# Moving the row normalisation of a macaron FFN-attention block from VectorE to ScalarE, with the order of the work refitted

## The chip, the cores and the metric

The kernel runs on one core of a Trainium2 chip. The metric is the device time of one launch in microseconds (us); of the kernel before there are three runs. Engines are named as in the profile: PE is TensorE, DVE VectorE, ACT ScalarE, POOL GpSimd, SP SyncE, which issues the transfers. L12 is line 12 of the kernel before, unless the text says that it is of the changed one.

## What is computed

The input x is 4 x 2048 x 256 float32. Three residual blocks follow one another, and each begins with a layer norm of the rows of x:

```python
x = x + 0.5 * ffn(layernorm(x), w_gate, w_up, w_down)
x = x + attention(layernorm(x), Wq, Wk, Wv, Wproj, lq1, lk1, lq2, lk2)
x = x + 0.5 * ffn(layernorm(x), w_gate, w_up, w_down)
# layernorm(x) = (x - mean) * rsqrt(var + eps), per row of 256
# ffn: every linear layer quantises input and weights to FP4 (E2M1) in
# blocks of 16: scale = max|x|/6, round x/scale to the grid, times scale;
# hidden size 704, silu(gate) * up
# attention: causal, 8 heads, two softmaxes per head whose difference
# (first - lam * second) weighs the values; q and k are RMS-normed and
# rotated, the output of a head is layer-normed
```

## The kernel before, in words

**Tiles.** A tile is 128 rows of x, a pair is two tiles, a chunk is four (512 rows). There are 16 chunks, four for each batch. The kernel makes four passes over a chunk: 0 is the first FFN, 1 the projections to q, k and v, 2 the output projection of attention, 3 the second FFN. `xb` holds five chunks of x; the load of chunk c+5 goes into the room of chunk c once that is stored. Weights are quantised, transposed and split into float16 high and low parts in a prologue, into which the first stages of chunk 0 are woven.

**From x to the matmul (passes 0, 1 and 3).** For a chunk, DVE makes mean and variance (`stats`, L1089 and L1092), POOL the reciprocal root (`rstd`, L905 to L916, six small steps on 128x4, once for a chunk and pass, 48 times). Then for each pair DVE writes the normed rows into `xq` (`norm_a`, L1104, two instructions of 128x256, one for each tile; 96 pairs, 192 instructions). In the FFN passes, the FP4 stages follow: `scale_x` on DVE (L1063, L1066, L1068), `divide_x` on POOL (L896), `square_x` on ACT (L979), `grid_x` and `points_x` on DVE (L1145, L1150), `dequant_x` on POOL (L923), and in all three passes `high_x` on ACT and `low_x` on POOL (L992, L930), and the transposing DMA `turn_x` from SP (L875). PE multiplies with the weights (L1299, `hidden`), ACT makes the tanh (L969), DVE the gate (L1122 to L1133), the hidden tile goes through the same FP4 stages (`hq`), PE multiplies again (L1312, `down`), and DVE adds to x (L1157).

**Attention.** For each chunk and each of four groups of heads: scores on PE (L1336), exp on ACT (L1036, two per step of 128 keys), on the diagonal a mask on POOL (L956), values on PE (L1354). Scores have two rooms of two PSUM banks each, or three for the (group, chunk) pairs listed in `WIDE`.

**What sets the order.** Every engine runs its own stream in order. A list scheduler, `Plan.order`, writes these streams when the kernel is built: at each step it places the stage that can start first, ties and near ties being settled by the table `DUE` (a due time for each kind of stage and each chunk). Its model has a cost for each kind (`COST`), gaps between a stage and the next (`LATE`, `AFTER`), and the stages in `PORT`, for which it lets DVE and POOL wait for one another. So every change of a cost or of `DUE` can move every stage on every engine; dependencies are kept by semaphores whatever the order. The model's numbers are no measurement, and none is used here.

**Lines to follow.** `norm_a` is added to DVE's stream in `quantise` (L435) and for pass 1 (L499), and run at L1093. SP's `store` is L862, its `load` L854, and before the load SP waits for the store of that room to have landed.

## Time and profile before

| what | value |
|---|---|
| time, median of 3 runs | 2159.77 us (2158.83 to 2162.08) |
| time of the profiled execution | 2159.3 us |
| span of the profiled execution | 2157.6 us |
| instructions | 39254 |
| granted TensorE clock, mean | 0.975 of 2.4 GHz |
| PE, DVE, ACT, POOL busy | 1878.2, 1688.2, 1626.0, 1351.2 us |
| L1104 on DVE | 192 instructions, 152.4 us |

The span runs from the first instruction to the last; the time adds what lies around it, here 1.7 us. Busy times are those of one execution, with overlaps counted once, and a DVE or POOL instruction that is held up after it has begun counts as busy. That is why a shape that always does the same work can have very different durations.

### The profile page before, as it was taken

What the parts mean: (1) busy time and instruction counts of PE and PEld (TensorE: products, weight loads), DVE (VectorE), ACT (ScalarE), POOL (GpSimd) and SP (SyncE); (2) the same over time, 40 slices, a digit from 0 to 9 for tenths busy, and PEclk for the clock granted to TensorE, in tenths of its full rate; (3) what the DMA queues carried; (4) which work ended last, traced back from release to release, by engine and by line L of the source; (5) the groups of instructions that cost most, each with busy time, mean ns of one, the idle gap of its engine ahead of it and who ended that gap; (6) DMA issues with size and microseconds to landing.
All of it is one profiled execution on the core that took longest, in us unless ns stands there. A gap on an engine that the chain in (4) does not pass through costs nothing. (4 is left out here: it accounts for less than half of the span.)

```text
span 2157.6 us, 39254 instructions
## 1 busy us (share of the span) xinstructions
PE 1878.2 (87%) x13634; PEld 785.1 (36%) x13634; DVE 1688.2 (78%) x3516; ACT 1626.0 (75%) x2339; POOL 1351.2 (63%) x1343
## 2 busy tenths in 40 slices
PE   1766999998999898999998999999999889999965
PEld 1332434343333342444332333444442424342223
DVE  8899898897845899889954999998976769841285
ACT  2334888877887788787889788777878778889942
POOL 6677776766645676776753677876764656641154
PEclk9898999999999999999999999999999989999988
DMA  4123543425221445332421444333521342320013
GB/s 125 31 54 69 86 82 63 87 44 93 49 48 35 71 68 103 61 85 46 79 58 24 73 78 86 62 72 71 90 46 43 59 79 55 72 48 17 11 33 70
DMA packets 477492, 136.15 MB, mean 63 GB/s; under 512 B 458224, under 2 KB 477040, under 8 KB 477296
## 3 DMA queue, kind: packets, MB, share of 16 engines
q1 hardware_dynamic: 477296, 133.65, 32.6%
q8 instruction: 110, 1.80, 0.4%
q14 instruction: 86, 0.70, 0.1%
HBM read 11.96 MB, written 8.39 MB: 9 GB/s over the span
## 5 line engine op out<-in xcount | busy, mean ns | idle before, releaser
L1036 ACT ACTIVATE probs<-psum 128x1024 f32<-128x1024 f32 (+3 forms) x1280 | 1071.7, 918 | 113.7 <-PE psum L1336 91.7
L1354 PE MATMUL psum_o<-probs,v_sb 128*32 128x512 f32 (+3 forms) x5120 | 570.3, 541 | 16.6 <-POOL probs L956 13.7
L1299 PE MATMUL psum<-w_gu_T,xT 128*128 128x512 f16 (+1 forms) x2304 | 507.7, 369 | 58.1 <-DVE qscale L1066 14.7
L1336 PE MATMUL psum<-q_stack,k_stack 64*128 64x512 f16 (+3 forms) x2560 | 386.6, 353 | 78.3 <-ACT probs L1036 59.5
L1299 PEld LDWEIGHTS psum<-w_gu_T,xT 128*128 128x128 f16 x2304 | 212.6, 99 | 331.6 <-issue 58.0
L1312 PE MATMUL psum<-w_down_T,hT 128*128 128x256 f16 x2176 | 269.1, 280 | 40.0 <-DMA hT<-h 14.1
L956 POOL TENSOR_SCALAR_AFFINE_SELECT probs<-probs 128x512 f32<-128x512 f32 x256 | 179.7, 709 | 160.3 <-ACT probs L1036 159.3
L1336 PEld LDWEIGHTS psum<-q_stack,k_stack 64*128 64x128 f16 x2560 | 99.4, 93 | 486.9 <-ACT probs L1036 374.1
L923 POOL TENSOR_TENSOR hq<-grid,qscale 128x704 f32<-128x704 f32 x128 | 187.0, 1462 | 126.2 <-DVE grid L1150 126.2
L969 ACT ACTIVATE hq<-psum,tanh_scale 128x512 f32<-128x512 f32 (+1 forms) x256 | 144.0, 563 | 150.9 <-PE psum L1299 143.6
L1312 PEld LDWEIGHTS psum<-w_down_T,hT 128*128 128x128 f16 x2176 | 210.6, 100 | 107.5 <-issue 31.1
L930 POOL TENSOR_TENSOR h<-hq,h 128x704 f16<-128x704 f32 x128 | 202.6, 1583 | 67.6 <-ACT h L992 67.2
L896 POOL TENSOR_TENSOR hq<-hq,rscale 128x704 f32<-128x704 f32 x128 | 188.6, 1474 | 78.8 <-DVE rscale L1068 78.3
L1354 PEld LDWEIGHTS psum_o<-probs,v_sb 128*32 128x32 f32 x5120 | 117.7, 109 | 245.5 <-issue 167.2
L930 POOL TENSOR_TENSOR x<-xq,x 128x512 f16<-128x512 f32 x128 | 160.6, 1256 | 69.0 <-ACT x L992 68.8
L1145 DVE SCALAR_TENSOR_TENSOR hq<-grid,hq 128x704 f32<-128x704 f32 x128 | 145.0, 1135 | 31.3 <-ACT grid L979 30.2
L1104 DVE TENSOR_SCALAR xq<-xb,mean_var,rstd 128x256 f32<-128x256 f32 x192 | 152.4, 841 | 17.4 <-POOL rstd L916 17.0
L1323 PE MATMUL psum<-w_qkv_T,xT 128*128 128x512 f16 (+1 forms) x768 | 144.4, 335 | 24.5 <-DMA xT<-x 8.4
L1150 DVE SCALAR_TENSOR_TENSOR grid<-grid,hq 128x704 f32<-128x704 f32 x128 | 149.8, 1173 | 0.7
L992 ACT ACTIVATE h<-hq 128x704 f16<-128x704 f32 x128 | 102.2, 798 | 47.1 <-POOL hq L923 34.4
L979 ACT ACTIVATE grid<-hq 128x704 f32<-128x704 f32 x128 | 101.7, 798 | 37.9 <-POOL hq L896 37.3
L1157 DVE SCALAR_TENSOR_TENSOR xb<-psum,down_scale,xb 128x256 f32<-128x256 f32 x128 | 58.9, 461 | 80.6 <-PE psum L1312 80.3
(118 smaller groups left out, 2319.4 us busy)
## 6 DMA issues: line engine op xcount, KB each, us to landing
xb<-L_attn_x SPq DMA_DIRECT2D x16, 512.0 KB, 4.0
out<-xb SPq DMA_DIRECT2D x16, 512.0 KB, 3.1
xT<-x SPq DMA_TRANSPOSE x128, 3.1
hT<-h SPq DMA_TRANSPOSE x128, 3.5
k_stack<-st SPq DMA_TRANSPOSE x64, 3.2
q_stack<-st SPq DMA_TRANSPOSE x64, 3.3
k_stack<-L_ffn_w_down SPq DMA_DIRECT2D x1, 704.0 KB, 4.1
k_stack<-L_ffn_w_gate SPq DMA_DIRECT2D x1, 512.0 KB, 5.2
```

Source lines behind the costliest of these rows:

```text
L896: nc.gpsimd.tensor_tensor(by_block(a), by_block(a), rscale[:, i, 0:nb].unsqueeze(2).broadcast_to([P, nb, QB]), ALU.mult).then_inc(scaled_r ...
L923: nc.gpsimd.tensor_tensor(by_block(a), by_block(g), qscale[:, i, 0:nb].unsqueeze(2).broadcast_to([P, nb, QB]), ALU.mult).then_inc(quantise ...
L930: nc.gpsimd.tensor_tensor(low, buffers(kind, key)[0], high, ALU.subtract)\
L956: nc.gpsimd.affine_select(out=blk, in_=blk, compare_op=ALU.is_ge, fill=0.0, base=0, pattern=[[0, 4], [1, P]], channel_multiplier=-1)\
L1036: nc.scalar.activation(probs[:, s % 3, 2 * u:2 * u + 2, q0:CHUNK], psum[:, plan.pairs[s, u]:plan.pairs[s, u] + 2, q0:CHUNK], ACT.Exp, scal ...
L1104: last = nc.vector.tensor_scalar(a[:, j * C:(j + 1) * C], xb[:, t % XB, :], mean_var[:, slot, i, 0:1], rstd[:, slot, i:i + 1], ALU.subtrac ...
L1145: nc.vector.scalar_tensor_tensor(a, g, GRID_BASE, a, ALU.add, ALU.add).then_inc(grid_ready, 1)
L1150: nc.vector.scalar_tensor_tensor(points(e[1], e[2:]), g, GRID_BASE, a, ALU.add, ALU.subtract)\
L1299: last = nc.tensor.matmul(bank(e)[:, 0:hi - lo], xs[:, x, t % 2, k, :], w_gu_T[:, w, k, lo:hi], start=n == 0, stop=n == len(parts) - 1)
L1312: last = nc.tensor.matmul(bank(e)[:, 0:C], hs[0:n, k, :], w_down_T[0:n, w, :], start=i == 0, stop=i == len(parts) - 1)
L1336: last = nc.tensor.matmul(psum[:, plan.pairs[s, u] + j, q0:CHUNK], k_stack[half, at, h, kt % NTC * P:(kt % NTC + 1) * P], q_stack[half, c ...
L1354: last = nc.tensor.matmul(psum_o[at:at + VD, q0:CHUNK], v_sb[:, kt // NTC % SLOTS * NTC + kt % NTC, 2 * g + u, :], probs[:, s % 3, 2 * u + ...
```

## The change

The norm becomes two ACT instructions with a scale and a bias per row: `x * rstd + offset`, where `offset = -mean * rstd` is made by POOL in two added steps of 128x4 after `rstd`. In `rstd`, the last product is no longer the end: a semaphore `mean_negated` counts the negated means, `early_rstd` the rstd, and `rstd_ready` is given after the offset. `scale_x` on DVE and `high_x` on ACT wait for `early_normed` as before, now counted in ACT's order.

In the scheduler: `norm_a` is on "scalar" with a cost of 1090 instead of 540, out of `PORT`, and the second pair of a chunk is also said to need the first; `rstd` costs 3400 instead of 2780; a load that follows a store on SP is counted from the end of the store (`AFTER`), where it was counted from the end of its issue. `WIDE` has 43 pairs of group and chunk instead of 35, and all rows of `DUE` have new numbers. In the prologue, the four norms of chunk 0 stand before ACT's third weight square instead of before DVE's `scale_x`.

```diff
 DUE = {
...
-WIDE = {0: (1, 5, 8, 9, 10, 12, 13, 14, 15), 1: (0, 1, 2, 3, 5, 6, 7, 13, 14, 15), 2: (3, 6, 8, 9, 11, 13, 14, 15), 3: (1, 5, 7, 10, 11, 13, 14, 15)}
+WIDE = {0: (1, 2, 3, 5, 6, 7, 10, 13, 14, 15), 1: (1, 2, 3, 4, 5, 6, 8, 11, 13, 14, 15), 2: (0, 2, 3, 5, 7, 9, 11, 12, 13, 14, 15), 3: (1, 2, 3, 4, 6, 7, 9, 10, 11, 13, 15)}
...
-            mask=640, norm_a=540, norm_heads=690, norm_qk=685, points_h=890, points_x=690,
+            mask=640, norm_a=1090, norm_heads=690, norm_qk=685, points_h=890, points_x=690,
...
-            read_v=470, rms=4170, rope=1940, rope_add=1270, rstd=2780, scale_x=1295, square_h=795,
+            read_v=470, rms=4170, rope=1940, rope_add=1270, rstd=3400, scale_x=1295, square_h=795,
...
-         ("head_stats", "norm_heads"): 35, ("rope", "rms"): 35, ("norm_a", "scale_x"): 35}
+         ("head_stats", "norm_heads"): 35, ("rope", "rms"): 35, ("store", "load"): 50, ("norm_a", "scale_x"): 35}
...
-            dequant_h=0, low_h=0, rope_add=0, low_qk=0, mask=0, norm_a=0)
+            dequant_h=0, low_h=0, rope_add=0, low_qk=0, mask=0)
...
-            add(norm, "vector", at("norm_a"), needs, takes, frees)
+            add(norm, "scalar", at("norm_a"), needs, takes, frees)
...
-            quantise("x", pair, [("rstd", *stats)], [("xu", pair)], [("stats", stats)] if i else [])
+            quantise("x", pair, [("rstd", *stats), ("norm_a", "x", pas, pair[1] - 1) if i else None], [("xu", pair)], [("stats", stats)] if i else [])
...
-                    nc.gpsimd.tensor_tensor(rstd[:, slot, :], t, y, ALU.mult).then_inc(rstd_ready, 1)
+                    n, o = EARLY_RSTD[e], offset[:, slot, :]
+                    nc.gpsimd.tensor_scalar(o, mean_var[:, slot, :, 0], -1.0, None, ALU.mult)\
+                        .then_inc(mean_negated, 1)
+                    nc.gpsimd.tensor_tensor(rstd[:, slot, :], t, y, ALU.mult).then_inc(early_rstd, 1)
+                    pool.wait_ge(mean_negated, n + 1)
+                    pool.wait_ge(early_rstd, n + 1)
+                    nc.gpsimd.tensor_tensor(o, o, rstd[:, slot, :], ALU.mult).then_inc(rstd_ready, 1)
...
+                    for j in range(2):
+                        t = 2 * p + j
+                        i = t % NTC
+                        last = nc.scalar.activation(a[:, j * C:(j + 1) * C], xb[:, t % XB, :], ACT.Identity,
+                                                    bias=offset[:, slot, i:i + 1], scale=rstd[:, slot, i:i + 1])
+                    last.then_inc(early_normed, 1)
...
-                        last = nc.vector.tensor_scalar(a[:, j * C:(j + 1) * C], xb[:, t % XB, :],
-                                                       mean_var[:, slot, i, 0:1], rstd[:, slot, i:i + 1],
-                                                       ALU.subtract, ALU.mult)
-                    last.then_inc(early_normed, 1)
...
-                    vector_stages(dve, first["norm_a"] + first["scale_x"])
+                    vector_stages(dve, first["scale_x"])
...
+                        if i == 2:
+                            scalar_stages(act, first["norm_a"])
```

**Where it moves instructions.** ACT in the prologue: the first stages of the kernel. L1744 and, in the changed kernel, L1756 are the squares of the three weight matrices, L1003 is the norm. Before:

```order
L1744 ACT_TABLE_LOAD
L1744 ACTIVATE probs<-k_stack 128x1536 x3
L979 ACTIVATE psum<-xq 128x512 x2
L1754 ACTIVATE w_gu_T<-psum,hq 128x512 x2
L1754 ACTIVATE w_gu_T<-psum,hq 128x192 x2
```

and in the changed kernel:

```order
L1756 ACT_TABLE_LOAD
L1756 ACTIVATE probs<-k_stack 128x1536 x2
L1003 ACTIVATE xq<-xb,offset,rstd 128x256 x4
L1756 ACTIVATE probs<-k_stack 128x1536
L990 ACTIVATE psum<-xq 128x512 x2
```

The four norms of chunk 0 now stand between the second and the third square. ACT's stream has one table load in either kernel.

DVE in 54:216, at the second chunk. `hq<-hq,psum` is the gate, `psum<-xq` to `rscale<-qscale` is `scale_x`, `hq<-grid,hq` and `grid<-grid,hq` are the grid steps of a hidden tile. Before:

```order
L1104 TENSOR_SCALAR xq<-xb,mean_var,rstd 128x256 x2
L1122 SCALAR_TENSOR_TENSOR hq<-hq,psum 128x512
L1145 SCALAR_TENSOR_TENSOR hq<-grid,hq 128x704
L1127 SCALAR_TENSOR_TENSOR hq<-hq,psum 128x512
L1150 SCALAR_TENSOR_TENSOR grid<-grid,hq 128x704
L1063 TENSOR_REDUCE psum<-xq 128x32
L1066 TENSOR_SCALAR qscale<-psum 128x32
L1068 RECIPROCAL rscale<-qscale 128x32
```

and in the changed kernel:

```order
L1132 SCALAR_TENSOR_TENSOR hq<-hq,psum 128x512
L1088 TENSOR_REDUCE psum<-xq 128x32
L1091 TENSOR_SCALAR qscale<-psum 128x32
L1093 RECIPROCAL rscale<-qscale 128x32
L1088 TENSOR_REDUCE psum<-xq 128x32
L1091 TENSOR_SCALAR qscale<-psum 128x32
L1093 RECIPROCAL rscale<-qscale 128x32
L1155 SCALAR_TENSOR_TENSOR hq<-grid,hq 128x704
L1137 SCALAR_TENSOR_TENSOR hq<-hq,psum 128x512
```

The norm is gone from the stream, and `scale_x`, which waits for it, stands directly behind gate steps, with grid steps of a hidden tile behind it. On PE, 72 of the 768 projection matmuls (L1323) and 234 of the 2304 `hidden` ones stand ahead of the first scores before, 96 and 264 in the changed kernel.

SP around the first store (`out<-xb`) and load (`xb<-L_attn_x`). Before:

```order
L875 DMA_TRANSPOSE xT<-x 128x8x128
L862 DMA out<-xb 128x4x256
L854 DMA xb<-L_attn_x 128x4x256
L875 DMA_TRANSPOSE xT<-x 128x8x128 x3
L875 DMA_TRANSPOSE hT<-h 128x11x128 x2
```

and in the changed kernel:

```order
L880 DMA_TRANSPOSE xT<-x 128x8x128
L867 DMA out<-xb 128x4x256
L880 DMA_TRANSPOSE xT<-x 128x8x128
L859 DMA xb<-L_attn_x 128x4x256
L880 DMA_TRANSPOSE xT<-x 128x8x128 x3
```

One transposition has come between the two. This is so for one of the 11 loads before and for five in the changed kernel.

## Rows read from the trace of the kernel before

**Rows 1.** The page: busy time, share of the span, instructions of each engine.
```profile
PE 1878.2 (87%) x13634; PEld 785.1 (36%) x13634; DVE 1688.2 (78%) x3516; ACT 1626.0 (75%) x2339; POOL 1351.2 (63%) x1343
```

**Rows 2.** Windows of the span: start and end, length, busy us per engine, PEclk, DMA.
```profile
54.00:216.00 162.00, 108.80 (x522) 54.29 (x522) 148.73 (x295) 63.88 (x110) 113.21 (x114) 0.85 0.27 51
216.00:2052.00 1836.00, 1696.25 (x12712) 690.07 (x12712) 1418.93 (x3018) 1515.98 (x2158) 1145.12 (x1145) 0.99 0.34 63
2052.00:2158.00 106.00, 63.52 (x366) 33.22 (x362) 75.33 (x138) 32.01 (x52) 55.19 (x48) 0.85 0.25 53
1944.00:2052.00 108.00, 99.07 (x800) 27.92 (x798) 22.12 (x63) 104.42 (x129) 17.33 (x26) 1.00 0.06 14
```

**Rows 3.** Windows of L1104 alone: start and end, length, DVE busy (x count).
```profile
54.00:216.00 162.00, 23.13 (x24) 0.85 0.27 51
216.00:2052.00 1836.00, 121.47 (x160) 0.99 0.34 63
540.00:702.00 162.00, 9.18 (x12) 1.00 0.21 43
1620.00:1728.00 108.00, 6.79 (x10) 0.98 0.26 52
1944.00:2052.00 108.00, 1.38 (x4) 1.00 0.06 14
```

**Rows 4.** L1104: durations in ns, least, median, most.
```profile
L1104 DVE TENSOR_SCALAR xq<-xb,mean_var,rstd x192: 315/718/2995, 24.0 to 2091.4; 128x256 f32<-128x256 f32 x192
```

**Rows 5.** Timeline at 807: start, duration, engine, line [idle before it <- releaser].
```profile
807.37 4.25 DVE L1104 TENSOR_SCALAR xq<-xb,mean_var,rstd 128x256 f32<-128x256 f32 x4 [0.29 <-POOL rstd L916]
808.33 1.33 POOL L935 TENSOR_TENSOR roped<-roped,rope_b 128x512 f32<-128x512 f32 x1
813.67 1.47 PE L1323 MATMUL psum<-w_qkv_T,xT 128*128 128x512 f16 x6 [2.42 <-DVE qscale L1066]
```

**Rows 6.** Lines on ACT: count, busy us, mean ns; then two in a row (timeline).
```profile
L1758 ACT ACTIVATE w_qkv_T<-hq 128x256 f16<-128x256 f32 x2 | 0.7, 406 | 0.0
L979 ACT ACTIVATE psum<-xq 128x512 f32<-128x512 f32 x64 | 39.6, 619 | 32.6 <-POOL xq L896 22.9 <-DVE rope_b L1181 3.8 <-DVE hq L1122 1.7
L1007 ACT ACTIVATE rope_b<-psum,att_scale 128x512 f32<-128x512 f32 x64 | 44.2, 691 | 28.6 <-POOL roped L935 15.4 <-PE psum L1323 13.1
L1754 ACT ACTIVATE w_proj_T<-psum,hq 128x256 f16<-128x256 f32 x2 | 0.9, 474 | 0.0
...
59.07 0.87 ACT L1754 ACTIVATE w_proj_T<-psum,hq 128x256 f16<-128x256 f32 x2
```

**Rows 7.** Lines on POOL: the first step of rstd.
```profile
L905 POOL TENSOR_SCALAR var<-mean_var 128x4 f32<-128x4 f32 x48 | 14.7, 307 | 81.7 <-DVE mean_var L1092 79.6
```

**Rows 8.** Timeline of the prologue, POOL, ACT and DVE.
```profile
17.93 1.64 POOL L916 TENSOR_TENSOR rstd<-root_t,root 128x4 f32<-128x4 f32 x1
22.36 1.48 ACT L1744 ACTIVATE probs<-k_stack 128x1536 f32<-128x1536 f32 x1 [5.28 <-POOL k_stack L1534]
23.97 3.96 DVE L1104 TENSOR_SCALAR xq<-xb,mean_var,rstd 128x256 f32<-128x256 f32 x4
```

**Rows 9.** Waits of PE in 216:2052: us in total, times, longest.
```profile
PE psum L1336 <- ACT probs L1036: 58.8, 138, 1.4
PE psum_o L1354 <- POOL probs L956: 13.3, 22, 1.6
PE psum L1336 <- DVE hq L1133: 5.6, 4, 2.2
```

**Rows 10.** Waits of SP and of DVE for the transfers of a chunk.
```profile
SPq L854 <- DMA out<-xb: 27.2, 11, 2.8
DVE stat L1089 <- DMA xb<-L_attn_x: 29.1, 10, 6.7
```

**Rows 11.** Timeline of the tail: the last four norms.
```profile
2087.89 3.86 DVE L1104 TENSOR_SCALAR xq<-xb,mean_var,rstd 128x256 f32<-128x256 f32 x4
```

**Rows 12.** L1036, the exps: durations in ns, first and last start.
```profile
L1036 ACT ACTIVATE probs<-psum x1280: 362/1021/1369, 212.1 to 2057.2; 128x1024 f32<-128x1024 f32 x128, 128x512 f32<-128x512 f32 x21, 128x256 f32<-128x256 f32 x17, 128x768 f32<-128x768 f32 x17
```

More of the change, by code:

```diff
@@ L498, in whole_plan @@
                 norm = ("norm_a", "x", *pair)
-                add(norm, "vector", of_pair("norm_a", *pair), [("rstd", 1, c), ("norm_heads", "x", 2, NTC * (c - 2) // 2 - 1) if c >= 3 else None],
+                add(norm, "scalar", of_pair("norm_a", *pair), [("rstd", 1, c), ("norm_a", "x", 1, pair[1] - 1) if i else None,
+                     ("norm_heads", "x", 2, NTC * (c - 2) // 2 - 1) if c >= 3 else None],
                     [(rings_of(*pair)[0], pair)], [("stats", (1, c))] if i == NTC - 2 else [])
@@ L696, in macaron_kernel @@
         early_normed = sem("early_normed")
+        mean_negated = sem("mean_negated")
+        early_rstd = sem("early_rstd")
         bank_full = [sem(f"bank_full{i}") for i in range(BANKS)]
@@ L739, in macaron_kernel @@
         QUANT = ordinals(order["vector"], ("quant_h", "scale_x"))
-        EARLY_NORM = ordinals(order["vector"], ("norm_a",))
+        EARLY_NORM = ordinals(order["scalar"], ("norm_a",))
+        EARLY_RSTD = ordinals(order["gpsimd"], ("rstd",))
         DIVIDE = ordinals(order["gpsimd"], ("divide_x", "divide_h"))
@@ L980, in scalar_stages @@
                         .then_inc(full(e)[0] if e[1] == "x" else square_done, 1)
+                elif e[0] == "norm_a":
+                    pas, p = e[2:]
+                    slot = STAT[pas, 2 * p // NTC] % STATS
+                    a = buffers("x", (pas, p))[0]
+                    before = last_low("x", (pas, p))
+                    if before:
+                        act.wait_ge(low_ready, before)
+                    act.wait_ge(rstd_ready, RSTD["rstd", pas, 2 * p // NTC] + 1)
+                    for j in range(2):
[4 more added lines that the diff above has]
+                    last.then_inc(early_normed, 1)
                 elif e[0] in ("high_x", "high_h"):
@@ L1092, in vector_stages @@
                         nc.vector.bn_aggr(mean_var[:, slot, i, :], stat6[:, i, :]).then_inc(var_ready, 1)
-                elif e[0] == "norm_a":
-                    pas, p = e[2:]
-                    slot = STAT[pas, 2 * p // NTC] % STATS
-                    a = buffers("x", (pas, p))[0]
-                    before = last_low("x", (pas, p))
-                    if before:
-                        dve.wait_ge(low_ready, before)
-                    dve.wait_ge(rstd_ready, RSTD["rstd", pas, 2 * p // NTC] + 1)
-                    for j in range(2):
-                        t = 2 * p + j
-                        i = t % NTC
-                        last = nc.vector.tensor_scalar(a[:, j * C:(j + 1) * C], xb[:, t % XB, :],
-                                                       mean_var[:, slot, i, 0:1], rstd[:, slot, i:i + 1],
-                                                       ALU.subtract, ALU.mult)
-                    last.then_inc(early_normed, 1)
                 elif e[0] == "scale_x":
```

63 lines of the change are left out of this document (32 added, 31 removed), and 136 rows, old and new, of the table DUE.

## The prediction

> **What bounds the kernel now.** I read the page's busy line first [rows 1]: PE 87%, DVE 78%, ACT 75%, POOL 63% of 2157.6 us. No engine is full over the whole span, so the question is which is full where. The windows answer it [rows 2]. Up to 54 us the weights are prepared. In 54:216 the first chunks go through the MLP with no attention beside it: DVE is busy 148.73 of 162 us (92%), PE 108.80 (67%), ACT 63.88 (39%), POOL 113.21 (70%). That stretch is DVE's. In 216:2052 attention and MLP run side by side: PE 1696.25 of 1836 us (92%), ACT 1515.98 (83%), DVE 1418.93 (77%). PE is nearest to full, and its 140 us of idle time are what can be won. In 2052:2158 the last MLP chunks drain through hand-offs between all engines, DVE 75.33 of 106 us.
>
> The operation that moves is L1104. It costs DVE 23.13 us in 54:216 and 121.47 us in 216:2052 [rows 3], 3.96 us for four in the prologue [rows 8] and 3.86 us for four in the tail [rows 11], 152.4 us in all, 794 ns of DVE time for each of the 192. Its single durations are 315 ns at least, 718 at the median, 2995 at most [rows 4], for one shape. What stretches it is seen at 807.37 [rows 5]: four of them take 4.25 us while POOL runs additions from SBUF one after another, and PE's projection at 813.67 has stood 2.42 us for a DVE step queued behind them. Advanced Engine Details and Errata in the Trainium skill (VectorE Performance Modes) says that VectorE's second SBUF port is shared with GpSimd and that two-port instructions and GpSimd's block each other. The trace agrees: the same 256 elements take 315 ns or over 1 us, beside a busy POOL.
>
> **The change, part by part.**
>
> *DVE loses L1104*: 192 instructions, 152.4 us.
>
> *ACT gains 192 ACTIVATEs* with a scale and a bias read from SBUF. The trace has none with two such operands. From below: 128x256 with neither takes 406 ns [rows 6]. Each operand: at 128x512, none takes 619 ns and one takes 691 [rows 6], so 72 ns. Two give 406 + 144 = 550 ns. Two in a row overlap: a pair of one-operand 128x256 takes 0.87 us where one takes 474 ns [rows 6], so 0.08 us less than the sum. A pair is then 2 x 0.55 - 0.08 = 1.02 us, 96 pairs 98 us. From both sides: 0.81 us a pair without any surcharge (78 us), and 1.38 us, the price of the one-operand 128x512 twice (133 us). I take 98, since the shape and the surcharge both have a row. ACT goes from 1626 to 1724 us (80%). ScalarE: Activation LUTs in the Trainium skill (What ACT_TABLE_LOAD costs) has 186 ns + 0.833 ns per element and 93 ns per pointer operand, which would be 585 ns for one; an estimate by it is about 5 us more over the kernel.
>
> *POOL gains two steps per chunk and pass*, 48 x 2 instructions of 128x4, as L905 is (307 ns) [rows 7]: 96 x 0.307 = 29 us, 0.6 us each time. POOL is busy 63% and its order is packed around other waits, so nothing of this is on the path, except that a norm's operands come some 0.6 us later. If POOL were full, it would cost the 29 us.
>
> *Prologue.* L1104 ran at 23.97 for 3.96 us, although rstd was there at 19.57 [rows 8]: DVE was in its weights until then. ACT had stood idle for the 5.28 us before 22.36. The new order puts the four norms ahead of ACT's third weight square: 19.6 + 0.6 + 2.0 = 22.2, about when that square is released. DVE can go on to the scaling steps 3.9 us sooner. After it DVE waits for POOL's weights in part; I count 2 of the 3.9 us.
>
> *54:216.* DVE's work falls by 23.1 us, from 148.7 to 125.6. If DVE kept its 13.3 us of idle time, the stretch would be 23 us shorter. But a norm is now a hand-off, POOL to ACT to DVE, and scale_x on DVE waits for it with gate and grid steps queued behind. ACT has the room: 63.9 us and 12 pairs are 76 us. I let DVE's idle time grow by half, 13.3 to 20: the stretch becomes 146 us, **16 us less**. Bounds: 0 and 23. PE's order now has 96 instead of 72 projection matmuls ahead of its first scores (in the section on the change), so this is not bought by leaving work for later; it only means that the first exp comes less early than the stretch shrinks.
>
> *216:2052.* PE's 140 us of idle time: 58.8 before scores for ACT and 13.3 for POOL's mask [rows 9]; the other 67.7 lie in small groups, most of them waits for DVE, the largest 5.6 us. DVE's load here falls from 77% to 71%, and the 4 us blocks as in [rows 5] vanish. I take a quarter of the 67.7, **17 us less**; bounds 0 and 67.7. Against it, 80 pairs, 82 us, enter ACT, which goes from 83% to 87%. Where ACT is the bound they show in full. The pure case is 1944:2052, ACT 104.42 of 108 us [rows 2]. With the other stretches that are thin in MLP, 12 norms in 540:702, 10 in 1620:1728, 4 in 1944:2052 [rows 3] and as many in 1080:1188, these are 30 norms, 15 pairs, **15 us more**. Elsewhere the exps have slack and I count none; if that cover is gone, it is the rival below. The new WIDE table gives three rooms of scores to 43 of 64 head groups of a chunk, where it was 35. PE's 58.8 us arise when both rooms wait for ACT, and if they came from the 29 narrow ones in equal parts, 8 of them turning wide would save 16 us. A third room doesn't make ACT faster, so I take a quarter, **4 us less**.
>
> *Store and load.* SP stood 27.2 us in 11 waits of the load for the store before it, and DVE 29.1 us in 10 waits for the rows of x [rows 10]. The new order places a transposition between the two in 5 of 11 cases, 1 before. The DVE waits lie in PE's busy middle. I count 0; bounds 0 and 5 us less.
>
> *Tail.* Four norms took 3.86 us on DVE, of which the first pair, half of it, stood ahead of everything that follows [rows 11]. Now 0.6 us on POOL and one pair of 1.02 us on ACT stand there; DVE is also free for its other steps: **1 us less**.
>
> **Sum:** 2 + 16 + 17 - 15 + 4 + 1 = 25 us less. The profiled execution has a span of 2157.6 us and a time of 2159.3, 0.5 below the median of 2159.8. I predict **2135 us**. What a measurement of this kernel can tell from no change is about 0.2%, 4 us.
>
> **The rivals.**
>
> *ACT becomes the bound (slower).* In 216:2052 each pair stands in ACT's order among exps with a median of 1.02 us [rows 12], and PE has two or three rooms of scores. A norm that has become ready late holds the exps behind it. For it: the scores already wait 58.8 us for ACT [rows 9]. Against: ACT is idle 320 us there. If all 80 pairs reach PE, that is 82 us more instead of 15. Break-even with my gains of 40 us is at half of them. At 60% they cost 49 us against those 40, which makes **2169 us**. By the rule of ScalarE: Activation LUTs (Rules for kernel authors), plain multiplies and adds belong on VectorE. By the shortest row, 315 ns, the move would indeed trade 192 x 0.315 = 60 us of DVE for 98 us of ACT; then 8 us would go from 54:216 in place of 23, and this rival would be the likeliest. The 794 ns of DVE time that each takes in these rows speak against the rule here.
>
> *The gain is given back (no change).* PE is 92% busy in the middle; its idle time may move from DVE's account to ACT's, and what the head wins is lost while chunks wait for their place. Head 18, middle -15, refitted order neither way: **2157 us**.
>
> *DVE was worse than it looks (much faster).* All of 23 + 4 in the head, half of the 67.7 in the middle, and ACT's pairs hidden: 61 us, **2099 us**.
>
> *The change doesn't do what it says.* A second function on ACT might force table loads. ACT's order has one table load, as before. I give this nothing.
>
> **How the numbers follow.** Forecast (2120 to 2152) 0.54; no change (2151 to 2164) 0.19, of which 0.07 lie below 2155.5; slower 0.16 (up to 2185); much faster (below 2120) 0.11. The range that leaves out about a fifth, a little of the slow side and most of the very fast: 2112 to 2166. Faster 0.72, same 0.12, slower 0.16.
>
> **What would show it.** Right: DVE near 1536 us and ACT near 1724; norms on ACT near 550 ns with little spread; the first exp, at 212.1 now [rows 12], near 195; PE's waits for DVE in the middle well below 60 us in sum. Wrong: the first exp comes no earlier (then DVE wasn't the head's bound); PE's wait for ACT before scores well above 75 us (the slower rival); POOL above 1400 us, or DVE idle before L1088 for ACT by tens of us (the hand-off is dearer than I have it).

## The result, and the profile after

The changed kernel takes 2111.47 us (median of 4 runs, 2110.53 to 2114.67), beside 2160.93 us for the kernel before on the same chip. The ratio is 0.9773, 95% interval 0.9756 to 0.979: 49.5 us less, where 25 were forecast. The time lies just under the range that was given. The profiled execution took 2114.67 us with a span of 2112.9; it was the longest of the four.

The page of the changed kernel, its busy line, answers to [rows 1]:

```profile
PE 1863.1 (88%) x13634; PEld 784.6 (37%) x13634; DVE 1550.5 (73%) x3324; ACT 1706.1 (81%) x2531; POOL 1374.2 (65%) x1439
```

DVE has lost 137.7 us, ACT has 80.1 more, POOL 23.0 more. PE's count is the same; its busy time is 15.1 us less, and its idle time fell from 279.4 to 249.8 us. Both together make the 44.7 us between the spans. PE's granted clock was higher, 0.983 in the mean of the span against 0.975, and its busy time is shorter in the same ratio (0.992 both). So a third of the 44.7 us is PE's own time for the same matmuls.

Windows of the changed kernel, columns as in [rows 2] (the last one ends with the kernel):

```profile
54.00:216.00 162.00, 118.66 (x646) 59.35 (x644) 148.19 (x308) 85.77 (x151) 135.05 (x137) 0.89 0.33 61
216.00:2052.00 1836.00, 1692.41 (x12716) 692.71 (x12715) 1323.44 (x2889) 1583.97 (x2324) 1162.38 (x1236) 0.99 0.35 63
2052.00:2113.00 61.00, 39.05 (x218) 22.75 (x215) 37.52 (x62) 17.04 (x26) 34.27 (x25) 0.84 0.36 73
```

In 54:216 DVE is as full as before (148.19 against 148.73 us). The relief was not turned into idle time: PE did 646 matmuls in that stretch, where it did 522. DVE is still the fullest engine of the head, it only gets more done there. The granted clock was 0.89 where it had been 0.85.

The lines that answer to [rows 4, 12], durations in ns and first and last start, then the norm's line with its busy time and mean:

```profile
L1003 ACT ACTIVATE xq<-xb,offset,rstd x192: 583/599/887, 21.7 to 2050.6; 128x256 f32<-128x256 f32 x192
L1061 ACT ACTIVATE probs<-psum x1280: 361/1024/1330, 204.9 to 2021.2; 128x1024 f32<-128x1024 f32 x128, 128x512 f32<-128x512 f32 x21, 128x256 f32<-128x256 f32 x17, 128x768 f32<-128x768 f32 x17
...
L1003 ACT ACTIVATE xq<-xb,offset,rstd 128x256 f32<-128x256 f32 x192 | 105.4, 618 | 21.1 <-POOL offset L927 14.7 <-POOL x L941 6.2
```

One norm lasts 599 ns at the median, 583 at least. Norms that follow one another overlap, so the 192 take 105.4 us together. They overlap with ACT's other instructions too, so ACT's busy time rose by 80.1 us only; in the same way DVE lost 152.4 us of norms and 137.7 of busy time. The spread of [rows 4] (315 to 2995 ns) is gone. The exps start 7.2 us earlier (204.9 against 212.1) and end 36.0 us earlier (2021.2 against 2057.2).

PE's waits in 216:2052, the rows that answer to [rows 9] (us in total, times, longest), and one of DVE over the whole span:

```profile
PE psum L1346 <- ACT probs L1061: 62.0, 129, 1.6
PE psum_o L1364 <- POOL probs L967: 10.6, 21, 1.7
PE psum L1309 <- DVE hq L1143: 4.7, 3, 3.0
...
DVE psum L1088 <- ACT xq L1003: 48.8, 13, 16.4
```

The scores wait for ACT little more than before (62.0 against 58.8 us), although 164 norms now stand in ACT's order in that stretch. All rows of that view with DVE as the releaser sum to 33.1 us, 48.2 before, and all with ACT to 68.2, 60.5 before. The window is the same for both kernels, but in the changed one it takes in 31 us behind the last exp; the next paragraph compares equal work instead. DVE itself stands 48.8 us for the norms in 13 waits, 16.4 us the longest: the new hand-off.

**Where the 44.7 us of the span arise.** I compare the two traces where PE has done the same amount of matmul work (each kind of matmul counted with its mean duration of before). The changed kernel is ahead by 3.6 us at PE's first `hidden` matmul (58.8 against 62.4), by 20.7 where the kernel before stands at 216 us (17 to 23 in the 40 us around it, since the two orders differ), by 36.1 at 2058 us, just behind the last exp, and by 44.7 at the end. The stretches of equal work between these points, columns as in [rows 2], the kernel before first:

```profile
59.40:215.90 156.50, 103.62 (x496) 50.51 (x496) 145.49 (x287) 58.52 (x97) 111.57 (x110) 0.85 0.28 53
215.90:2057.80 1841.90, 1701.24 (x12759) 691.37 (x12757) 1421.70 (x3024) 1521.78 (x2168) 1149.18 (x1150) 0.99 0.34 63
2057.80:2157.60 99.80, 58.63 (x324) 32.00 (x316) 72.56 (x132) 26.21 (x42) 51.23 (x43) 0.84 0.27 56
```

```profile
55.80:195.20 139.40, 97.58 (x499) 49.40 (x499) 127.82 (x264) 69.64 (x122) 117.66 (x123) 0.88 0.32 58
195.20:2021.70 1826.50, 1693.32 (x12757) 693.23 (x12754) 1315.90 (x2863) 1587.52 (x2328) 1163.32 (x1230) 1.00 0.35 63
2021.70:2112.90 91.20, 57.86 (x320) 31.58 (x316) 64.07 (x129) 27.82 (x45) 50.74 (x44) 0.88 0.31 61
```

So 3.6 us come up to the first `hidden` matmul, 17.1 in the head behind it, 15.4 in the 1840 us of the middle and 8.6 in the tail. In the middle PE's waits for DVE fell from 48.2 to 22.4 us and those for POOL from 13.3 to 10.0; its waits for ACT rose from 61.2 to 69.2 and those for transfers from 8.1 to 15.7; short gaps and waits for nothing that the profile shows are 5.8 us more; its own time fell by 7.9 us, at a granted clock of 1.00 against 0.99. In the tail PE's waits for transfers fell from 22.2 to 13.9 us. PE's waits there, two rows of the kernel before and the largest of the changed one:

```profile
PE psum L1299 <- DMA xT<-x: 11.3, 2, 7.0
PE psum L1312 <- DMA hT<-h: 10.9, 3, 5.5
...
PE psum L1322 <- DMA hT<-h: 13.9, 4, 4.8
```

### The profile page after: what moved, and what is told of

Same layout as the page of the kernel before. It is cut to its first block and busy times, and to the rows that moved or that the text cites. A ratio compares the mean times of both kernels' runs of the same rounds, so it can differ in the third digit from the quotient of the medians.

```text
span 2112.9 us, 39423 instructions
## 1 busy us (share of the span) xinstructions
PE 1863.1 (88%) x13634; PEld 784.6 (37%) x13634; DVE 1550.5 (73%) x3324; ACT 1706.1 (81%) x2531; POOL 1374.2 (65%) x1439
## 5 line engine op out<-in xcount | busy, mean ns | idle before, releaser
L1346 PE MATMUL psum<-q_stack,k_stack 64*128 64x512 f16 (+3 forms) x2560 | 384.8, 352 | 81.8 <-ACT probs L1061 62.4
L1309 PEld LDWEIGHTS psum<-w_gu_T,xT 128*128 128x128 f16 x2304 | 213.7, 99 | 314.0 <-issue 48.2
L980 ACT ACTIVATE hq<-psum,tanh_scale 128x192 f32<-128x192 f32 (+1 forms) x256 | 143.0, 561 | 106.7 <-PE psum L1309 105.5
L901 POOL TENSOR_TENSOR hq<-hq,rscale 128x704 f32<-128x704 f32 x128 | 187.5, 1466 | 62.5 <-DVE rscale L1093 62.0
L941 POOL TENSOR_TENSOR x<-xq,x 128x512 f16<-128x512 f32 x128 | 156.5, 1226 | 77.7 <-ACT x L1017 77.4
L1333 PE MATMUL psum<-w_qkv_T,xT 128*128 128x512 f16 (+1 forms) x768 | 141.9, 331 | 13.6 <-DVE xb L1167 6.6
L1167 DVE SCALAR_TENSOR_TENSOR xb<-psum,down_scale,xb 128x256 f32<-128x256 f32 x128 | 59.8, 468 | 105.2 <-PE psum L1322 104.7
L1003 ACT ACTIVATE xq<-xb,offset,rstd 128x256 f32<-128x256 f32 x192 | 105.4, 618 | 21.1 <-POOL offset L927 14.7
```

Source lines behind the costliest of these rows:

```text
L901: nc.gpsimd.tensor_tensor(by_block(a), by_block(a), rscale[:, i, 0:nb].unsqueeze(2).broadcast_to([P, nb, QB]), ALU.mult).then_inc(scaled_r ...
L941: nc.gpsimd.tensor_tensor(low, buffers(kind, key)[0], high, ALU.subtract)\
L980: nc.scalar.activation(buffers("h", h[1:3])[0][:, lo:hi], bank(h)[:, 0:hi - lo], ACT.Tanh, scale=tanh_scale[:, 0:1]).then_inc(tanh_done, 1)
L1309: last = nc.tensor.matmul(bank(e)[:, 0:hi - lo], xs[:, x, t % 2, k, :], w_gu_T[:, w, k, lo:hi], start=n == 0, stop=n == len(parts) - 1)
L1346: last = nc.tensor.matmul(psum[:, plan.pairs[s, u] + j, q0:CHUNK], k_stack[half, at, h, kt % NTC * P:(kt % NTC + 1) * P], q_stack[half, c ...
```

## The experiments

The experiments are built on both kernels with one thing changed: each of the 384 transposing DMAs is a plain copy of the same tile, so the products that follow work on untransposed data. `plain_b4` and `plain_a4` are these two bases; the others change one of them further. Where an order is said to be kept, the planner runs unchanged and the result is edited after it, so every other instruction keeps its place on its engine. The kernel before, run beside each group of experiments, took 2159.1 to 2160.6 us, so times of different groups can be compared to some 2 us.

### The bases

```
-  sp.dma_start_transpose(to, halves(kind, key)...)
+  sp.dma_start(to, halves(kind, key)...)
```

> The kernel before with each of the 384 transposing transfers replaced by a plain copy of the same tile, so that rows are not transposed and the output isn't the reference's; nothing else changes. It is the base of the experiments. If the plain copies land within 1 us of the 3.1 to 3.5 us of the transposing ones, the time stays within 1% of 2161 us.

> The changed kernel with the same replacement. If the transposing transfers play no part in the gain, its ratio to the kernel before with plain copies is 0.977 within 0.004, as for the two whole kernels. If they do, the ratio is above 0.985 or below 0.969.

Measured: 2155.27 us (10 runs, ratio to the kernel before 0.998, 0.997 to 0.9989) and 2101.68 us (ratio 0.9731, 0.9712 to 0.9749). The step between them, 53.6 us or a ratio of 0.975, is that of the change within its interval, so the bases stand for the two kernels. The transposing transfers are not quite without a part: PE's waits for transfers in 216:2052 rise by 7.6 us (8.1 to 15.7) with the change in the whole kernels and by 2.9 (1.3 to 4.2) in the bases, about as much as the gain of the bases is larger.

### What a norm costs on each engine, alone and beside POOL

A program of its own: 12 norms on DVE alone, 12 beside POOL's multiplications of 128x512, 24 on ACT of which the last 12 beside POOL, and 12 bn_stats on DVE beside POOL.

> A small program in place of the kernel: twelve norms of 128x256 on DVE alone, twelve POOL products of 128x512 alone, both together, twelve norms on ACT alone and beside POOL, and twelve statistics of 128x256 on DVE beside POOL. If the 794 ns of a norm on DVE come from POOL's instructions, it is under 350 ns alone and near the length of a POOL instruction beside them, while the statistics and the norm on ACT (583 ns at least in the changed kernel) keep their times beside POOL. If not, all keep their times.

The timeline of this program (start, duration of the group, line, count):

```profile
8.91 3.96 DVE L73 TENSOR_SCALAR dve_out<-xb,pair 128x256 f32<-128x256 f32 x12 [8.91 <-DMA xb<-L_attn_x]
13.02 29.96 POOL L56 TENSOR_TENSOR pool_out<-pa,pb 128x512 f32<-128x512 f32 x24 [11.27 <-DVE dve_out L73]
27.74 15.39 DVE L73 TENSOR_SCALAR dve_out<-xb,pair 128x256 f32<-128x256 f32 x12 [14.87 <-POOL pool_out L56]
...
44.53 12.05 ACT L92 ACTIVATE act_out<-xb,pair 128x256 f32<-128x256 f32 x24
...
65.35 4.02 DVE L82 BATCH_NORM_STATS2 stat_out<-xb 128x6 f32<-128x256 f32 x12 [22.22 <-POOL pool_out L56]
```

A norm on DVE takes 330 ns alone (3.96 / 12) and 1283 ns beside POOL (15.39 / 12), where one POOL multiplication follows another every 1268 ns: one norm gets through for each POOL instruction. Two batches of 12 on POOL took 29.96 us with the norms beside the second, and a batch without any takes 14.70: POOL loses 0.56 us on 12, or 4%. ACT's norms come every 502 ns (12.05 / 24) with or without POOL. bn_stats on DVE, over the same 256 elements, takes 4.02 us for 12 beside POOL, about what 12 norms take alone. So ACT's price is steady, and DVE's depends on what POOL does.

### Each half of the change alone, the order kept

`act_old_order` is the kernel before in its own order, with each norm moved from DVE's list into ACT's at the start that the plan had for it, and POOL's two steps added. `dve_new_order` is the reverse: the changed kernel in its own order, each norm back in DVE's list, POOL's two steps kept.

```
   order = plan.order()
+  moved = [e for e in order["vector"] if e[0] == "norm_a"]
+  order["vector"] = [e for e in order["vector"] if e[0] != "norm_a"]
...
+  to = order["scalar"]
...
+  for e in moved:
+      if e not in LEAD:
+          n = next((i for i, o in enumerate(to) if o not in LEAD and plan.start[o] > plan.start[e]), len(to))
+          to.insert(n, e)
```

> Plain copies; the kernel before with every engine's order kept, only the 192 norms taken out of DVE's stream and put into ACT's at their planned times, with POOL's two added steps. Theory relief (the gain is DVE's 152 us of norms, off an engine that sets the pace in the head and holds others for 2 to 4 us at a time in the middle): most of the gain is there without any refit, 28 to 50 us below the kernel before with plain copies. Theory refit (the new DUE and WIDE tables carry the gain, wherever the norm runs): within 12 us of it. A third, that norms between exps only pay with an order that allows for them: 5 us or more above it, and PE's wait for ACT before scores well above 62 us.

> Plain copies; the changed kernel with every engine's order kept, only the 192 norms taken out of ACT's stream and put into DVE's at their planned times (POOL's two added steps stay). Theory relief: the gain is lost, 40 us or more above the changed kernel with plain copies, DVE busy above 1690 us. Theory refit: within 15 us of it.

Measured: act_old_order 2158.92 us (10 runs), ratio 0.9999 to the kernel before, 0.9988 to 1.0009; that is 3.7 us above its base. dve_new_order 2209.75 us, ratio 1.0229: 108 us above its base. Neither the move nor the order alone gains anything. Theory relief, most of the gain without any refit, is refuted by the first run. Theory refit has the time of the first run (within 12 us) and is refuted by the second (within 15 us was its figure). The third has the mechanism, 87.6 us of waits where it said well above 62, and its time is short of it, 3.7 us for 5 or more.

| | order of before | new order |
|---|---|---|
| norm on DVE | 2155.3 | 2209.8 |
| norm on ACT | 2158.9 | 2101.7 |

PE's largest waits in 216:2052, first of the base of before, then of act_old_order, then of the base of after, then of dve_new_order:

```profile
PE psum L1336 <- ACT probs L1036: 57.6, 137, 1.4
PE psum_o L1354 <- POOL probs L956: 12.8, 21, 1.6
PE psum L1336 <- DVE hq L1133: 5.6, 4, 2.2
PE psum L1323 <- DVE qscale L1066: 5.5, 4, 2.4
```

```profile
PE psum L1356 <- ACT probs L1071: 87.6, 165, 3.5
PE psum_o L1374 <- POOL probs L977: 9.5, 16, 1.3
PE psum_o L1374 <- ACT probs L1071: 6.3, 8, 1.8
PE psum L1319 <- DVE hq L1142: 3.2, 5, 2.0
```

```profile
PE psum L1346 <- ACT probs L1061: 61.7, 127, 1.7
PE psum_o L1364 <- POOL probs L967: 10.2, 21, 1.7
PE psum L1309 <- DVE hq L1143: 5.0, 3, 3.0
```

```profile
PE psum L1372 <- ACT probs L1072: 50.5, 104, 2.9
PE psum L1335 <- DVE qscale L1102: 13.0, 9, 4.9
PE psum L1372 <- DVE qscale L1102: 10.7, 6, 3.3
```

Summed over all rows of this view, PE's waits in 216:2052 stand as follows: for DVE 53.3 us in the base of before, 27.4 in act_old_order, 40.1 in the base of after, 103.0 in dve_new_order; for ACT 59.5, 97.7, 65.7 and 55.5. (Of the 40.1 us only 25.8 lie ahead of the last exp, at 2008.9.) In the old order the move took 26 us of waits for DVE away and put 38 us of waits for ACT in their place. The new order has the one with little of the other. PE's own time for the same matmuls counts as well: 1888.1 us in the base of before, 1886.3, 1862.7 and 1889.8, at granted clocks of 0.970, 0.971, 0.981 and 0.967. These 25 us are part of the 59 between the two bases' spans (2157.0 and 2098.1); the move alone or the order alone has none of them.

The old order did gain in the head. Its exps as the trace's lines have them, the base of before and act_old_order:

```profile
L1036 ACT ACTIVATE probs<-psum x1280: 366/1022/1383, 213.1 to 2058.8; 128x1024 f32<-128x1024 f32 x128, 128x512 f32<-128x512 f32 x21, 128x256 f32<-128x256 f32 x17, 128x768 f32<-128x768 f32 x17
```

```profile
L1071 ACT ACTIVATE probs<-psum x1280: 361/1023/1383, 199.2 to 2067.4; 128x1024 f32<-128x1024 f32 x128, 128x512 f32<-128x512 f32 x21, 128x256 f32<-128x256 f32 x17, 128x768 f32<-128x768 f32 x17
```

It is 13.9 us ahead at the first exp and 8.6 us behind at the last one. The lead was 8.9 us at the 240th exp and gone by the 480th.

### Only the head's norms on ACT

```
+  on_act = lambda e: at_chunk[e[2], 2 * e[3] // NTC] < HEAD_NS     # 216000
-  moved = [e for e in order["vector"] if e[0] == "norm_a"]
+  moved = [e for e in order["vector"] if e[0] == "norm_a" and on_act(e)]
```

> The order of the kernel before as it was, plain copies for the transposes, and only the 32 normalisations planned before 216 us moved to ACT (with POOL's two extra steps for every chunk); the other 160 stay on DVE. With all 192 moved at this order (act_old_order) the first exponential came 13.9 us earlier (199.2 against 213.1), and the whole was 3.7 us slower. Theory A (in the head the relief of DVE is worth its full size, and the loss comes behind the head, where ACT's exponentials stand between PE's scores and products): the first exponential near 199, PE's waits for ACT from 216 to 2052 near 60 us as with the norm on DVE and not near 98, and the program near 2141, 14 us below plain_b4's 2155.3. Rival B (an order laid out for a late head gives the head start back by itself, at places where the engines wait for what is not late, whoever does the norm): first exponential near 199 too, but 2150 to 2157.

Measured: 2151.75 us (2146.99 to 2153.61), ratio 0.9959, 0.9943 to 0.9975: 3.5 us below its base, whose interval it just touches (0.997 to 0.9989), inside what rival B gave. The first exp stands at 199.1, and PE's waits for ACT in 216:2052 sum to 61.2 us, as theory A had it. But the lead shrinks all the same: 13.9 us at the first exp, 9.6 at the 240th, 8.3 at the 480th, 3.8 at the last. So a head that is 14 us shorter is worth 4 us at the last exp in an order that was laid out for a longer one. Where the 10 us go is settled in part only: in 216:2052 PE's waits for POOL are 3.6 us above the base (16.4 against 12.8), those for DVE and ACT 1.8 and 1.7 (55.1 against 53.3, 61.2 against 59.5).

### How much an engine's time is worth in each order

The norm is cut to 8 of its 256 columns wherever its room has been written before; the rest of the row keeps older values.

```
-  nc.vector.tensor_scalar(a[:, j * C:(j + 1) * C], xb[:, t % XB, :], ...)
+  w = 8 if before else C
+  nc.vector.tensor_scalar(a[:, j * C:j * C + w], xb[:, t % XB, 0:w], ...)
```

In the two kernels with the norm on ACT, the same cut is made in its `nc.scalar.activation`.

> The kernel before with plain copies, its normalisation on DVE cut to 8 of 256 columns for all but the first use of each room (the rest of the row keeps older values): DVE loses some 110 to 140 us of its 159, nothing is added on ACT. Theory F (in the old order DVE's relief is worth something and ACT's norms took it back): 15 to 40 us below plain_b4's 2155.3. Rival G (an order laid out around a norm on DVE can't use the relief): 2147 to 2157, and then only the head's share shows.

> act_old_order with the normalisation on ACT cut to 8 columns in the same way (ACT loses some 50 to 60 us of 104; its fixed part and POOL's two steps stay). Theory F: between dve_tiny_old and act_old_order's 2158.9, 10 to 25 us below it, and PE's waits for ACT from 216 to 2052 down from 98 to about 75 us. Rival G: within 5 us of act_old_order.

> The changed kernel with plain copies and the same cut of the normalisation on ACT. It tells what ACT's norms still cost in the order that was laid out for them. Theory F (the new order has put them where ACT had room): within 8 us of plain_a4's 2101.7. Rival H (ACT is the next bound, as the page's 81 per cent and the exponentials' share of the waits suggest): 15 us or more below it.

| kernel | norms' time on their engine | program | against its full norm |
|---|---|---|---|
| dve_tiny_old | DVE 159.2 to 135.4 us | 2138.76 | -16.5 |
| act_tiny_old | ACT 104.2 to 65.6 us | 2127.95 | -31.0 |
| act_tiny_new | ACT 105.5 to 66.7 us | 2096.47 | -5.2 |

The two cuts on ACT take the same 39 us of it away. In the old order that is worth 31.0 us, in the new one 5.2. This is the cause of the zero: taking the norm off DVE was worth at least 27 us in the old order (act_tiny_old is 27.3 us below the base with the norm on DVE, and still carries 65.6 us of norms on ACT), and the norms' full time on ACT took it back. Theory F named this and its range for act_tiny_old (10 to 25) was too small, and the run lies below dve_tiny_old where F had it above; the waits for ACT fell from 97.7 to 84.2 us, not to 75. Rival G (no use for the relief in the old order) and rival H (15 us or more below) are out.

dve_tiny_old did not do what I wrote. DVE lost 24 us, not 110 to 140, and these 24 were worth 16.5 of program. The norm's line in the base of before and with 8 columns:

```profile
L1104 DVE TENSOR_SCALAR xq<-xb,mean_var,rstd x192: 315/722/2892, 21.3 to 2093.1; 128x256 f32<-128x256 f32 x192
```

```profile
L1104 DVE TENSOR_SCALAR xq<-xb,mean_var,rstd x192: 193/651/2997, 24.0 to 2072.1; 128x8 f32<-128x8 f32 x186, 128x256 f32<-128x256 f32 x6
```

The least falls by 122 ns, the median by 71, the most not at all. Most of a norm's time on DVE in this kernel is not for its elements.

### Extra work on DVE in the new order

ACT's norm is kept, and 188 extra pieces of work that nobody reads stand on DVE at the norm's planned places: one bn_stats each, two, or the norm itself.

```
+  elif e[0] == "ghost":
+      dve.wait_ge(rstd_ready, RSTD["rstd", pas, 2 * p // NTC] + 1)
+      for j in range(2):
...
+          for k in range(1):       # range(2) in ghost_two, tensor_scalar in ghost_norm
+              ghosts[0] = done(nc.vector.bn_stats(ghost[:, 6 * k:6 * k + 6], xb[:, t % XB, :]))
+          wait(ghosts[0])
```

As the norm does, each piece waits for the rstd, and then for its own end. DVE's idle time before the pieces is 13.6 to 14.0 us in all three.

> The changed kernel's own order with ACT's norm kept, plain copies, and 188 extra DVE instructions at the norm's planned places: one bn_stats of xb into scratch that nobody reads (about 410 ns each, 77 us in all; it waits for rstd as the norm does). Theory C (the order has no room on DVE at these places, and what costs is DVE's time as such): about half of dve_new_order's 108 us, 2140 to 2160. Rival D (what costs is POOL's hold on a normalisation and what DVE then holds up; short instructions of fixed length fit into DVE's idle 530 us): within 20 us of plain_a4's 2101.7.

> As ghost_one with two bn_stats at each place, about 820 ns, 154 us in all, as long as the normalisation was on DVE (867 ns, 158 us) but an instruction that POOL did not lengthen in norm_cost2. Theory C: dve_new_order's 108 us or somewhat more, since ACT keeps its 105 us: 2205 to 2240. Rival D: 2110 to 2150.

> As ghost_two with the normalisation itself (tensor_scalar of xb by mean and rstd into scratch) in place of the bn_stats, which POOL's products lengthen (867 ns in dve_new_order). Theory C: equal to ghost_two within 15 us, since both take DVE's time alike. Rival D: 50 us or more above ghost_two, near 2210 to 2240. A third, E (dve_new_order was slow because DVE's norm hands over later than ACT's and everything behind it waits, not because DVE is taken): all three ghosts within 20 us of 2101.7, since nobody waits for a ghost's result.

| kernel | extra DVE time | program | against 2101.7 | PE's waits for DVE, 216:2052 |
|---|---|---|---|---|
| ghost_one | 78.8 us | 2144.12 | +42.4 | 62.5 |
| ghost_two | 139.9 us | 2206.85 | +105.2 | 97.6 |
| ghost_norm | 153.9 us | 2221.55 | +119.9 | 106.7 |
| dve_new_order | 158.3 us | 2209.75 | +108.1 | 103.0 |

Theory C holds: the cost follows the time that DVE is taken, 0.54 us of program per us of DVE in the first step and about 0.75 with the whole (105.2 / 139.9, 119.9 / 153.9). From ghost_one to ghost_two, 61.1 us more on DVE cost 62.8, the full price. It does not matter whether the time is bn_stats, which POOL does not stretch, or a norm that it does (rival D is out), and nobody waits for a ghost's result, so E falls too. What POOL's hold does is to make a norm 2.5 times as long as it would be alone (158.3 / 192 = 824 ns of DVE in dve_new_order against 330); from there on it is time like any other.

DVE is idle for some 550 us of this kernel (2098.1 - 1549.7), and 79 us of extra work still cost 42. The share of the span says little here; the places at which the order puts the norm have no room.

### The planner's inputs, one at a time

Here the planner runs anew, with one of its inputs set back.

```
  no_load_rule:   -  ("store", "load"): 50,
  old_wide:       -  WIDE = (the new one)              +  WIDE = (that of before)
  old_due:        -  DUE, WIDE = (the new ones)        +  DUE, WIDE = (those of before)
```

> The changed kernel without the rule that a load counts from the end of its room's store plus 50, table and all else as changed; plain copies. Theory A (the rule moves only where SP's loads stand in the order, and a chunk's room is asked for long before it is read): within 5 us of plain_a4's 2101.7. Rival B (the table was fitted with the rule, and any change of the order's planning at fixed table costs tens of us): 2115 to 2140.

> The changed kernel with the WIDE list of the kernel before (which exponentials are taken two scores at a time), all else as changed; plain copies. The list shifts few exponentials between 512 and 1024 columns, and wider ones save ACT a fixed part each. Theory A (worth what the counts say): 2 to 8 us above plain_a4's 2101.7. Rival B (the order depends on it at large): 2115 or more.

> The changed kernel with its new stage costs, norm on ACT and load rule, but with the due-time table and the WIDE list of the kernel before; plain copies for the transposes. Theory A (what the gain needs is that the planner knows norm's engine and cost and keeps ACT's norms out of the way of its exponentials by itself): 2100 to 2125, most of the 54 us between plain_b4 and plain_a4. Rival B (the gain is in the refitted due times; without them the order stands about as in act_old_order): 2150 to 2175, with PE's waits for ACT from 216 to 2052 at 90 us or more.

Measured: 2181.12 us, 2239.36 and 2258.99, that is 79, 138 and 157 us above the base. I had the size of none by theory A, which had at most 23 us for any of them. The rivals' figures for no_load_rule and old_due (up to 38 and 73 us) were too small, and only that for old_wide, 2115 or more, holds. What I wrote of WIDE there was wrong too: the list sets how many rooms of scores there are, not how wide an exp is, and 896 of the 1280 exps have 1024 columns with either list. PE's wait for ACT before the scores in 216:2052 in the three, in the order of the diff above:

```profile
PE psum L1346 <- ACT probs L1061: 85.2, 177, 1.3
```

```profile
PE psum L1346 <- ACT probs L1061: 100.8, 186, 2.8
```

```profile
PE psum L1346 <- ACT probs L1061: 99.3, 195, 1.9
```

It was 61.7 us in the base. What a piece is worth by itself is not measured by these three: the rule for the load touches only a transfer on SP, yet taking it out changes the planner's decisions from there on: PE's order is the base's for the first 1990 matmuls, and of the 13634 places 8526 hold another kind. What they show is that due times fitted to one set of inputs lose more than the whole gain under another, that these three orders, which nobody fitted, lie 80 to 160 us above this one, and that of PE's waits the one for ACT before the scores grew most in each. The new planner with the old tables (old_due) is 104 us slower than the base of before. Theory A for old_due, that knowing the costs is enough for the planner, is refuted. The reverse, the new DUE and WIDE with the costs and stages of before, gives no kernel: its order has stages that wait for one another.

## Why the prediction was wrong

The sign was right, and so was the size of the head. The middle gave 15.4 us where I had 6, and the tail 8.6 where I had 1; these two are most of what is missing, and in neither had the refitted order a part of its own in my sum.

- **Prologue and 54:216, 2 + 16 us less.** At equal work 3.6 and 17.1 us: right in sum, in part by luck. DVE's busy time for this work fell by 17.7 us (145.5 to 127.8) and not by 23, and its idle time stayed at 11 us (156.5 - 145.5, 139.4 - 127.8) where I had it grow by half; the two errors cancel. The first exp stands at 204.9 and not near 195. 195 was the full shrinkage, against my own sentence that it comes less early than that, since 96 instead of 72 projection matmuls, and more of the MLP, now lie ahead of it.
- **216:2052, 17 + 4 us less and 15 more, 6 us less together.** This is the step that failed. At equal work the middle is 15.4 us shorter. Two terms were mis-sized. "15 norm pairs show in full on ACT", 15 us: PE's waits for ACT rose by 8.0 us (61.2 to 69.2), and taking 39 us off ACT's norms gives back only 5. "A quarter of the 67.7", 17 us: PE's waits for DVE fell by 25.8 (48.2 to 22.4). Two more had no term in the sum, and they nearly cancel: PE's own time for the same matmuls fell by 7.9 us, and its waits for transfers rose by 7.6. The 4 us for WIDE no run shows by itself; old_wide changes the whole order.
- **"Refitted order neither way".** I priced the move against ACT's load as it was spread before and gave the order no part of its own. act_old_order shows what my method priced: the old order with ACT's norms gains nothing, 38 us more of waits for ACT against 26 less for DVE. There my 15 us was too small. In the new order the same term is half of what I had. The order is not a third term beside relief and load: between the first and the last exp PE's waits for DVE fall by some 26 us in either order, but its waits for ACT rise by 38 us in 216:2052 of the old one and by 6 in the new one (65.7 against 59.5). I had counted it at zero.
- **Norm on ACT, 98 us.** 105.4 us measured, 599 ns for one at the median, and 1.10 us a pair (105.4 / 96) where I had 1.02. The surcharge for two operands, 144 ns, was 50 ns short. But ACT's busy time rose by 80.1 us only, since a norm overlaps with what stands beside it: ACT is at 1706 and not near 1724, and DVE for the same reason at 1550.5 and not near 1536. ScalarE: Activation LUTs in the Trainium skill (What ACT_TABLE_LOAD costs) has a fixed part, a part per element and a surcharge per pointer; an estimate by them is 585 ns for this form. The trace agrees (583 at least, 588 in the program of single norms). My "about 5 us more" was wrongly added: 35 ns more for each of 192 are 6.7 us.
- **POOL, 29 us.** Busy time rose by 23.0 us. ACT waited 14.7 us for the offset in 10 waits. In the prologue two of the steps took 1.70 and 1.79 us beside DVE, so the first norm started at 21.7 and not at 20.2. What that costs PE no run shows.
- **Store and load, 0.** DVE's wait for a chunk's rows is 14.2 us in 6 waits, 29.1 in 10 before [rows 10]. No run shows that PE gained by it: the one that takes the rule out changes the whole order.
- **Tail, 1 us.** 8.6 us were gained there. From the last exp to the end of the span it is 91.7 us, and was 100.4. The last norms now start at 2049.12, so they lie 28 us behind the last exp, where they lay 31 us behind it (2087.9 against 2057.2); PE's idle time there fell from 41.1 to 33.4 us. I had looked only at the norms. What went is the wait of two `hidden` matmuls for `xT<-x`, 11.3 us, and it went with the order: among the experiments it is 9.3 us in the base of before, 9.2 in act_old_order, 1.6 in dve_new_order and 0 in the base of after.
- **The rivals.** "ACT becomes the bound" is what happens in the old order, in mechanism (PE's waits for ACT up by 38 us, 0.8 us of program per us of norm on ACT) though not by that much in sum. "DVE was worse than it looks" was nearest in size, 2099 against 2111, and I had given it 0.11. It had the head at 27 and the middle at 34 us less with ACT's pairs hidden; the pairs were hidden in part, the head gave 20.7, the middle 15.4 and the tail 8.6. So its size is near for other reasons than it named.
- **The signs I named.** The rise of DVE's idle time before L1088 for ACT "by tens of us" was to tell against me: it is 48.8 us, and the kernel is faster than forecast. It was a bad sign: PE's waits for DVE, which are what such idle time could cost, fell all the same.
- **The rule against the change.** The rule of ScalarE: Activation LUTs in the Trainium skill (Rules for kernel authors), that plain multiplies and adds belong on VectorE, fits a norm alone in these runs, 330 ns against ACT's 502 ns apart. Beside POOL it is 1283 ns against 502, and the kernel, with 794 ns of DVE for a norm, lies between the two.

What stays open, and it is the largest rival left: whether due times fitted anew with the norm on DVE would have found part of the 54 us as well. dve_new_order and the ghosts say that this order cannot bear the norm on DVE; they don't say that no other could. The fitting itself was not tried, and neither was a norm on ACT in the order of before with due times fitted for it alone.

## What to carry to other kernels

When an operation moves to another engine, price it at the place it will have and not by the engine's share: here the same 39 us on ACT were worth 31 us in one order and 5 in another, and DVE with 550 us of idle time charged half or more of all that was added to it in this order. Try the move alone in the old order as well as in the new; a zero there can be a gain and a loss of like size, and shrinking the moved operation on its new engine separates them. In this kernel a table of due times belonged to the costs that it was fitted to: one rule, one list or the table itself set back cost 79 to 157 us. So whoever changes a cost, a rule or a list beside such a table has to fit again before the time tells what the change is worth. And PE's own time is no constant of the sum: the same 13634 matmuls took 1888 us in one base and 1863 in the other.

## What was not expected of the hardware

A normalisation on DVE beside a busy POOL takes as long as one POOL instruction, 1283 ns against POOL's 1268 in the program of single norms. Its width matters little: in the full kernel a norm takes 651 ns at the median when 186 of the 192 have 8 columns, and 722 when all have 256. dve_tiny_old has this line for those of 8 columns:

```profile
L1104 DVE TENSOR_SCALAR xq<-xb,mean_var,rstd 128x8 f32<-128x8 f32 x186 | 129.5, 747 | 19.5 <-POOL rstd L916 18.7 <-POOL x L930 0.9
```

On the same engine and the same source, bn_stats takes 410 ns beside POOL in that program and 414 in ghost_two. Cutting the norm to 3% of its width saved 24 of 159 us on DVE (15%) and 39 of 104 on ACT (37%). Moving it took all of it off DVE.

POOL is not always the one that goes on. In that program it lost 4%, but its two added steps of 128x4, 230 and 196 ns at the median, took 1.70 and 1.79 us in the changed kernel's prologue, each about as long as the DVE instruction that ran beside it, which reads two tensors from SBUF:

```profile
17.73 1.76 DVE L1644 SCALAR_TENSOR_TENSOR probs<-probs,k_stack 128x1536 f32<-128x1536 f32 x1
17.88 1.70 POOL L922 TENSOR_SCALAR offset<-mean_var 128x4 f32<-128x4 f32 x1
19.52 1.76 DVE L1645 SCALAR_TENSOR_TENSOR k_stack<-probs 128x1536 f32<-128x1536 f32 x1
19.55 1.79 POOL L924 TENSOR_TENSOR rstd<-root_t,root 128x4 f32<-128x4 f32 x1
```
